# RWKV-6 block on one core: decay totals first, queries scaled a level ahead, decay products by token halves, tanh arguments in strips

## What is computed

```python
xx  = x_prev - x
mix = tanh((x + xx * maa_x) @ maa_w1).reshape(b, t, 5, 32)      # maa_w1: 512 x 160
mw, mk, mv, mr, mg = einsum('btfe,fec->fbtc', mix, maa_w2)
xw, xk, xv, xr, xg = (x + xx * (maa_f + m_f) for each f)
r, k, v, g = xr @ Wr.T, xk @ Wk.T, xv @ Wv.T, silu(xg @ Wg.T)
w = time_decay + tanh(xw @ td_w1) @ td_w2                       # 512 x 64, 64 x 512
d = exp(-exp(w))
# per head (16 heads of 32): for every token
y = r_t @ (S + u * k_t^T v_t);   S = d_t * S + k_t^T v_t
x1 = layernorm(x + (groupnorm(y) * ln_g + ln_b) * g @ Wo.T)
h  = layernorm(gelu(x1 @ ternary(W_fc).T))                      # 512 -> 2048
out = layernorm(x1 + h @ ternary(W_proj).T)                     # 2048 -> 512
```

## Time and profile before

| | us |
|---|---|
| median of three runs | 3308.46 |
| profiled execution | 3307.6 |
| its span, first to last instruction | 3305.7 |
| PE busy | 3080.0 (93%) |
| DVE busy | 2449.2 (74%) |
| ACT busy | 1913.6 (58%) |
| POOL busy | 933.9 (28%) |
| mean granted TensorE clock | 0.982 of full |

### The profile page before, as it was taken

One profiled execution on the slowest core, in us unless ns is written; L12 is line 12 of the kernel. 1 busy time (PEld: TensorE's weight loads), 2 busy tenths in 40 slices (PEclk: granted clock), 3 DMA queues, 4 the chain that ended last, 5 costly groups with the idle time before them and its releaser, 6 DMA issues.

```text
span 3305.7 us, 98915 instructions
## 1 busy us (share of the span) xinstructions
PE 3080.0 (93%) x39133; PEld 2229.9 (67%) x39133; DVE 2449.2 (74%) x5172; ACT 1913.6 (58%) x3919; POOL 933.9 (28%) x825
## 2 busy tenths in 40 slices
PE   1899999999999999999999999999999999999997
PEld 0667666767666767666767666767666767666765
DVE  8467787777787777787777687777777777787777
ACT  0456566556566556566655566655566655566654
POOL 3223322223322223322233322233322233322232
PEclk9899999999999999999999999999999999999999
DMA  5000000000000000000000000000000000000000
GB/s 198 14 8 21 15 18 21 18 14 21 15 18 21 18 14 21 16 17 21 18 14 21 20 13 21 18 15 20 21 12 21 18 16 19 21 12 21 18 21 14
DMA packets 22741, 73.24 MB, mean 22 GB/s; under 512 B 3088, under 2 KB 3344, under 8 KB 20688
## 3 DMA queue, kind: packets, MB, share of 16 engines
q1 hardware_dynamic: 22352, 66.96, 5.9%
HBM read 50.17 MB, written 16.78 MB: 20 GB/s over the span
## 4 chain that ended last, share of the span: by engine, by line
PE 48%; DVE 27%; ACT 13%; issue 10%; DVEq 1%; DMA 1%; ACTq 0%; POOL 0%; SPq 0%; POOLq 0%
PE psP L393 10%; PE psP L425 7%; PE psF L637 5%; PE psP L591 5%; ACT HHI L820 4%; PE psF L618 4%; DVE HLO L1288 4%; ACT ARENA L661 3%; DVE ARENA L1138 3%; ACT GG L811 2%; DVE SUMS L1280 2%; DVE ARENA L1126 2%; PE psW L464 2%; PE psW L481 2%; DVE ARENA L1169 2%
## 5 line engine op out<-in xcount | busy, mean ns | idle before, releaser
L661 ACT ACTIVATE ARENA<-ARENA 32x512 f32<-32x512 f32 (+3 forms) x1026 | 581.1, 569 | 263.9 <-DVE ARENA L1114 202.1
L393 PE MATMUL psP<-ARENA,WALL 128*128 128x256 f32 x3072 | 688.0, 380 | 0.2 <-ACT ARENA L694 0.2
L393 PEld LDWEIGHTS psP<-ARENA,WALL 128*128 128x128 f32 x3072 | 574.4, 190 | 73.7 <-issue 0.7
L1288 DVE SCALAR_TENSOR_TENSOR HLO<-GG,FWB,HHI 128x128 f16<-128x128 f32 x1024 | 302.0, 357 | 368.1 <-ACT HHI L820 362.9
L618 PE MATMUL psF<-XHI,WFC 128*128 128x128 f16 x4096 | 487.0, 220 | 2.4 <-DVE ST L1306 2.1
L618 PE MATMUL psF<-XLO,WFC 128*128 128x128 f16 x4096 | 485.7, 219 | 0.0
L618 PEld LDWEIGHTS psF<-XHI,WFC 128*128 128x128 f16 x4096 | 400.4, 99 | 31.5 <-issue 26.3
L881 POOL TENSOR_TENSOR ARENA<-ARENA,XT 128x1024 f32<-128x1024 f32 x128 | 278.2, 2174 | 505.5 <-DVE ARENA L1059 505.5
L618 PEld LDWEIGHTS psF<-XLO,WFC 128*128 128x128 f16 x4096 | 401.4, 98 | 17.6 <-issue 10.3
L637 PE MATMUL psF<-WPJ,HHI 128*128 128x512 f16 x1024 | 405.7, 396 | 4.7 <-ACT GG L811 4.7
L637 PE MATMUL psF<-WPJ,HLO 128*128 128x512 f16 x1024 | 402.3, 393 | 0.0
(11 more groups left out here) (164 smaller groups left out, 5298.9 us busy)
## 6 DMA issues: line engine op xcount, KB each, us to landing
XT<-x_ch SPq DMA_DIRECT2D x33, 520.0 KB, 3.4
ARENA<-x_tok SPq DMA_DIRECT2D x32, 512.0 KB, 4.8
out<-OUT SPq DMA_DIRECT2D x64, 256.0 KB, 3.0
WALL<-w_all SPq DMA_DIRECT2D x5, 1024.0 KB, 15.9
...
```

The lines of the kernel that those rows point to most:

```text
L393: mm = pe.matmul(psP[:, P.bank(f"{name}{g}"), COLS * c:COLS * (c + 1)], WALL[:, w, k, 128 * (2 * g + c):128 * (2 * g + c + 1)], cc(XF[slot ...
L661: return act.activation(o, i, ACT.Copy)
L1288: e = dve.scalar_tensor_tensor(out=HLO[:, k, :], in0=GG[:, u % 2, 0, 128 * m:128 * (m + 1)], scalar=FWB[:, 0, k:k + 1], in1=HHI[:, k, :], ...
```

## The change

Five edits, of which the first moves the most.

1. **Totals first, queries a level ahead.** All six `TOT` products are made in one go (`totals`), as soon as D is ready, ahead of the copies with u (L1138). `scale_right` of a level is then issued ahead of `scale_left` of the level before it; the last `scale_right` (n = 32) comes ahead of the last `copy_predicated`, and the first `fold` after the second `copy_predicated` in place of the first.
2. **Decay's two products by token halves.** td1 writes tokens 0 to 127 into partitions 0 to 63 and tokens 128 to 255 into partitions 64 to 127 of one bank: eight matmuls of 128 columns. TZ becomes 128x128. td2 takes each half from its own 64 partitions (TD2 is loaded twice, one DMA more) and writes the two halves into two banks in turn. ACT's exponentials become eight of 128 columns in place of four of 256.
3. **w1b in four strips.** Each of its four matmuls becomes four of 64 columns, each into its own 32 partitions; ACT's tanh becomes four of 32x64, and is moved behind the first mix's high copies. POOL's low parts wait for TMH alone, and for TMBH only ahead of the last two.
4. **Moments ahead of the last down.** In F_SEQ `st` now stands ahead of `pj` for the second token half, so that `moments` of it doesn't wait for the last quarter of `down`.
5. In `alone` PE's `stats(1)` is put ahead of the last quarter of `down`.

The diff, cut:

```diff
 F_SEQ = [(f"{n}_{p}", e) for p in range(PAIRS)
-         for n, e in (("fc0", "act"), ..., ("fc3", "act"), ("pj", "product"), ("st", "stats"))]
+         for n, e in (("fc0", "act"), ..., ("fc3", "act"))
+         + ((("pj", "product"), ("st", "stats")) if p == 0 else (("st", "stats"), ("pj", "product")))]
...
+                        for q in range(4):
+                            mm = pe.matmul(ps[MIXR * q:MIXR * (q + 1), 0:CH], W1[:, k, 4 * MIXR:5 * MIXR],
+                                           cc(XF[1], k)[:, CH * q:CH * (q + 1)], ...)
...
                 for k in range(KC):
-                    mm = pe.matmul(psP[0:DECR, P.bank("td1"), 0:COLS], TD1[:, k, :], cc(XF[1], k), ...)
+                    for h in range(2):
+                        mm = pe.matmul(psP[DECR * h:DECR * (h + 1), P.bank("td1"), 0:128], TD1[:, k, :],
+                                       cc(XF[1], k)[:, 128 * h:128 * (h + 1)], ...)
...
+                for c in range(KC):
+                    for h in range(2):
+                        r = slice(DECR * h, DECR * (h + 1))
+                        mm = pe.matmul(psP[:, P.bank(f"td2{h}"), 128 * c:128 * (c + 1)],
+                                       TD2[r, 128 * c:128 * (c + 1)], TZ[r, :], start=True, stop=True)
...
                         for part in range(4):
+                            if part == 3 and p:
+                                stats(p)
                             down(j, p, part)
...
+            def mix_high(t, arguments, n):
+                act.wait_ge(tm_ready, M.read(t, "w1a"))
+                copy(TMH.bitcast(F32R), TMA[:, :]).then_inc(tm_rounded, 1)
+                high(t, 0)
+                act.wait_ge(arguments, n)
+                for q in range(4):
+                    e = act.activation(TMB[:, CH * q:CH * (q + 1)], ps[MIXR * q:MIXR * (q + 1), 0:CH], ACT.Tanh)
...
-                pool.wait_ge(tm_rounded, 2 * t + 4)
+                pool.wait_ge(tm_rounded, 2 * t + 3)
...
+                def totals():
+                    for i in range(NPL):
+                        t = TOT[2 ** i].rearrange("p (q two) -> p two q", two=2)
+                        if i:
+                            dve.wait_ge(tot_ready, NPL * it + i)
+                        dve.tensor_tensor(TOT[2 ** (i + 1)], t[:, 0, :], t[:, 1, :], ALU.mult).then_inc(tot_ready, 1)
...
                 for i, n in enumerate(LEVELS):
-                    if i:
-                        scale_right(i + 1, n)
+                    scale_right(i + 2, 2 * n)
                     scale_left(i + 1, n)
+                    if i + 2 < NPL - 1:
+                        queries(i + 2, 4 * n)
...
-                    if ffn and n == 2:
+                    if ffn and n == 4:
                         ffn.fold(0, 0)
-                scale_right(5, 32)
```

More of the change, by code:

```diff
@@ L408, in tile @@
                 pe.wait_ge(p_act, P.read(it, "td1"))
-                for g in range(2):
-                    P.wait_free(pe, it, f"td2{g}", first)
-                    for c in range(2):
-                        mm = pe.matmul(psP[:, P.bank(f"td2{g}"), COLS * c:COLS * (c + 1)],
-                                       TD2[:, 128 * (2 * g + c):128 * (2 * g + c + 1)], TZ[:, :], start=True, stop=True)
-                    mm.then_inc(p_full, 1)
+                for h in range(2):
+                    P.wait_free(pe, it, f"td2{h}", first)
+                for c in range(KC):
+                    for h in range(2):
+                        r = slice(DECR * h, DECR * (h + 1))
+                        mm = pe.matmul(psP[:, P.bank(f"td2{h}"), 128 * c:128 * (c + 1)], TD2[r, 128 * c:128 * (c + 1)], TZ[r, :],
+                                       start=True, stop=True)
+                        if c == KC - 1:
+                            mm.then_inc(p_full, 1)
                 if ffn:
@@ L582, in tile @@
                 pe.wait_ge(x_dve, X.read(it, "kv1"))
-                for name, lo, n in (("w1a", 0, 4 * MIXR), ("w1b", 4 * MIXR, MIXR)):
+                for name in ("w1a", "w1b"):
                     wait_free(name)
-                    tanh_argument(M_BANKS[M.bank(name)][0:n, 0:COLS], lo, n).then_inc(m_full, 1)
+                    tanh_argument(name).then_inc(m_full, 1)
                 pe.wait_ge(z_ready, 2 * it + 2)
@@ L691, in tile @@
                     act.wait_ge(p_full, P.full(it, f"td2{g}"))
-                    for c in range(2):
-                        k = 2 * g + c
-                        e = act.activation(cc(D, k), psP[:, P.bank(f"td2{g}"), COLS * c:COLS * (c + 1)], ACT.Exp,
+                    for k in range(KC):
+                        e = act.activation(cc(D, k)[:, 128 * g:128 * (g + 1)], psP[:, P.bank(f"td2{g}"), 128 * k:128 * (k + 1)], ACT.Exp,
                                            bias=PAR[:, k, DECAY:DECAY + 1])
@@ L792, in tile @@
                 act.activation(TMA[:, :], M_BANKS[M.bank("w1a")][:, 0:COLS], ACT.Tanh).then_inc(tm_ready, 1)
-                act.wait_ge(m_full, M.full(it, "w1b"))
-                act.activation(TMB[:, :], M_BANKS[M.bank("w1b")][0:MIXR, 0:COLS], ACT.Tanh).then_inc(tm_ready, 1)
-                mix_high(it)
+                mix_high(it, m_full, M.full(it, "w1b"))
             def feed_forward(j, before):
@@ L1141, in tile @@
                     e.then_inc(rb_dve, 1)
-                dve.wait_ge(d_ready, it + 1)
-                scale(0, 1)
+                dve.wait_ge(tot_ready, NPL * it + 6)
+                scale_right(0, 1)
+                scale_left(0, 1)
                 queries(0, 2)
@@ L1157, in tile @@
                 scale_right(1, 2)
+                queries(1, 4)
                 if ffn:
```

72 lines of the change are left out of this document (39 added, 33 removed).

## The result

The changed kernel takes 3374.74 us in the median of four runs (3372.47 to 3376.27), the kernel before 3308.74 beside it: the ratio is 1.02, with a 95% interval of 1.0182 to 1.0218. The prediction was 3302, with a range from 3280 to 3326. The profiled execution of the changed kernel has a span of 3371.7 us against 3305.7.

A forecast was written before the change was run, and what follows sets the result against it. DVE was taken to bound the levels and z to the tokens, PE the stretch from there to the next levels. 23 x (-0.5) + 8 x 0.65 - 1.2 + 1.0 = -6.5 us gave 3302, range 3280 to 3326.

The forecast's parts named there:

- w1b in strips: Ahead of Wo: PE saves about 1.25 us, then waits for z; with ACT's and POOL's new order, 0 on the path.
- rival 3: POOL's low parts collide with DVE around HLO: 0.7 us once a tile, 3324; twice, 3346; chance 0.13.
- w1b on PE: PE's w1b matmuls ahead of Wo: 1.91 us down to some 0.65, the saving of about 1.25 becoming a wait for z.
- td1, td2: Decay's products ahead of the tokens: about 1.05 us each, from 1.94 and 1.99; 0 on the path, hidden behind normalise.
- Moments: On DVE ahead of normalise: the wait of 0.31 us goes, but normalise starts no sooner; 0 of at most 0.31.
- Totals first: On DVE at the start of the levels: all totals ahead, so the copies with u start 2.2 us later.
- Queries ahead: DVE's stretch in the levels: 25.85 us for 26.34, clock full; 0.5 won, or 0.65 lost where it was already full.
- Tile 0 and the end: Tile 0's levels hide the totals, a gain of 1.2 us; in the last feed-forward the product is 1.0 late.
- Rival 4: PE's clock falls from Wo on, after new idle ahead of Wo and the tokens: 0.6 us a tile, 3320; chance 0.10.

The follow-up runs named there:

- f_norm_first: The kernel before with one change, DVE doing normalise ahead of moments: 3307.62 us (ratio 1.0002).
- g_moments: The kernel before with only moments ahead of the last down and, in the last feed-forward, the sums ahead of down's last quarter: 3310.35 us (ratio 1.0005).
- a_pool_waits: The changed kernel with one wait more, POOL starting its ten low parts only after the tile's last HLO group: 3317.69 us (ratio 1.0027).

## Why the prediction was wrong

**The step that failed** is in "w1b in strips": "POOL's earlier start lie[s] beside DVE's work", at 0, and its rival 3, which had the place right and the size and chance wrong. It allowed one low part getting in between two DVE instructions, "0.7 once a tile", at a chance of 0.13. The runs show three, at 0.50 to 0.53 each: 1.58 x 31 = 49. My evidence against it, that the two of `normalise` end 0.74 behind POOL's addition, doesn't bear on the question: behind that addition POOL had only one small instruction to run (FV, 128x1), no second large one. In f_norm_first POOL's addition does ask in the middle of two of DVE's, and gets in. The Trainium skill (SBUF — State Buffer, "SBUF: two separate sides") says that the one that starts first holds the ports for its instruction; the runs agree per instruction, but I read it as if a run of instructions held them. In two sequences that meet, the engines take turns, instruction by instruction.

**The rest, in the prediction's order.**
- *w1b on PE*: right, 1.35 us of idle ahead of Wo for 1.25.
- *td1, td2*: 1.19 and 1.16 for 1.05 each, hidden as said. The row groups of td2 do overlap: with 16 weight loads it takes 1.16, below the estimated 1.7 from the Trainium skill (TensorE: Matmul & The Clock Gate, Part 2) for loads that don't. By itself edit 2 costs 32 us, for a reason outside the working: late instructions.
- *Moments*: right, 0 in g_moments.
- *Totals first*: right in total, 2.19 for 2.2.
- *Queries ahead*: PE's order came as worked out, with idle times of 0.64, 0.98, 0.48 and 0.74 us ahead of levels 1, 4, 8 and 16 (foreseen 1.0, 0.7, 0.3 and 0.55), and the levels keep their clock. DVE's sum was mis-sized: 26.32 for 25.85. Against the tile with a full clock before it grew by 1.13, not 0.66. In steps from start to start: the totals cost 0.08 more than when they stood among the scalings, where I had allowed 0.4, and the last `scale_right` costs 0.61, as taken. But the three moved `queries` save 0.08 together and not 0.3 (a `scale_right` and a `queries` take 1.15 us as steps where they took 1.18), a `scale_left` ahead of `queries` takes a step of 0.72 where it took 0.61 ahead of a total, four times 0.11, and the steps behind the `copy_predicated` add another 0.11. So 23 tiles won nothing and 8 lost 1.15: +7.4, tile 0's gain taken off.
- *Tile 0 and the end*: tile 0 won 1.1 in the levels for 1.2, and 2.0 more behind XLO; the end cost 3.1 instead of 1.0, since the clock was at half there. The 2.48 us of idle ahead of the sums don't settle that by themselves: g_moments has them too, at a full clock and for 1.0. The sums took 1.01 for 0.61, and the last quarter, from 3361.68 to 3365.25, 3.57 for the 1.8 of my sum.
- *Rival 4* (the clock falls elsewhere) came true in 18 tiles, but as a consequence of the collision: without it they and the 6 us up to XLO are gone.

Of the 66 us of span a_pool_waits takes off 55, of which 53 lie behind z. The other 11 are 7.4 in the levels, 2.5 the other way behind XLO (2.0 of it in tile 0), and 5.9 at start and end, where the end explains 3.1; the start varied between 126.0 and 131.5 us over all these executions. The 2.8 us on the way to z stay open: PE's idle time "issue" in `values` is 15.8 us against 8.2 before, but a_pool_waits has 15.1 of it and no loss on that way.
